# Last combine of a two-layer transformer kernel: the first expert's product moved to ScalarE, the first sum to GpSimd, for three of four tiles

## What is computed

```python
x = x + _L1_ffn_ref(_layernorm(x, axis=-1), L1_ffn_W1, ..., L1_ffn_br)
# in it:
h = jax.nn.gelu(jnp.einsum('td,edp->etp', xf, W1) + b1[:, None, :])
y = jnp.einsum('etp,epd->etd', h, W2) + b2[:, None, :]
out = jnp.einsum('te,etd->td', router_weights, y)
```

## Time and profile before

| What | Value |
|---|---|
| median of 3 runs | 548.41 us |
| the profiled execution, whole | 552.02 us |
| its span, first to last instruction | 550.3 us |
| PE / DVE / ACT / POOL busy | 87% / 70% / 39% / 54% |
| first last-combine instruction starts | 537.31 us |
| last last-combine instruction starts | 547.66 us, lasts 0.35 us |

### The profile page before, as it was taken

How to read it: one execution, slowest core, us unless ns; L and a number is a source line. 1 busy time by engine, 2 the same in 40 slices (tenths; PEclk the granted TensorE clock), 3 DMA queues, 4 the chain that set the end, 5 groups by cost and what they waited for, 6 DMA issues and landing times.

```text
span 550.3 us, 11816 instructions
## 1 busy us (share of the span) xinstructions
PE 478.7 (87%) x3625; PEld 429.6 (78%) x3625; DVE 387.1 (70%) x1304; ACT 215.9 (39%) x503; POOL 296.6 (54%) x310
## 2 busy tenths in 40 slices
PE   7658999999999697898777999999999789999950
PEld 6447998899987587788655988888888689989950
DVE  3655899888874435555358899999999546666637
ACT  3525666555652433333233343434434114333320
POOL 5346578888844224555523457676675623545440
PEclk9979999999999979999898999999999979999985
DMA  7999950000004622221020001010000012222117
GB/s 212 365 331 358 367 190 20 16 16 20 22 20 138 252 62 70 67 65 57 25 68 10 20 21 31 29 35 16 16 16 20 20 49 70 58 66 65 47 33 213
DMA packets 42931, 49.18 MB, mean 89 GB/s; under 512 B 7809, under 2 KB 28636, under 8 KB 42871
## 3 DMA queue, kind: packets, MB, share of 16 engines
q1 hardware_dynamic: 36991, 39.57, 22.8%
q0 software_dynamic: 4544, 8.44, 4.7%
q10 hardware_dynamic: 1336, 0.43, 0.4%
HBM read 20.97 MB, written 28.35 MB: 90 GB/s over the span
## 4 chain that ended last, share of the span: by engine, by line
PE 59%; POOL 12%; DVE 11%; issue 5%; DMA 3%; ACT 3%; SPq 2%; another core or an unknown queue 2%; POOLq 0%; DVEq 0%; ACTq 0%
PE ps L1581 12%; PE ps L1592 9%; POOL qr L498 5%; PE ps L1542 5%; PE ps L1519 5%; POOL rows L491 4%; PE ps L1496 3%; PE ps L1571 3%; PE ps L1447 3%; PE ps L1534 2%; PE ps L1544 2%; PE ps L1275 2%; PE ps L1360 1%; PE ps L1510 1%
## 5 line engine op out<-in xcount | busy, mean ns | idle before, releaser
L545 POOL DMA_INDIRECT ys<-ysbs,xs x78 | 77.8, 998 | 101.4 <-DVE ysbs L1233 43.0
L1581 PE MATMUL ps<-xsT,wups 128*128 128x128 f32 x624 | 87.1, 284 | 2.3 <-DVE big L1216 2.3
L1581 PEld LDWEIGHTS ps<-xsT,wups 128*128 128x128 f32 x624 | 78.8, 198 | 3.3 <-ACT xsT L717 2.4
L498 POOL TENSOR_TENSOR qr<-qsm,mhalf 128x16 f32<-128x16 f32 x16 | 47.5, 2966 | 3.0 <-DVE qsm L853 2.9
L491 POOL DMA_INDIRECT rows<-pays,slots x32 | 33.8, 1055 | 24.6 <-DVE slots L994 17.2
L519 POOL DMA_INDIRECT rows<-pays,slots x32 | 32.7, 1022 | 20.3 <-DVE slots L1059 14.5
L510 POOL TENSOR_TENSOR pp<-pp,rden 128x1232 f32<-128x1232 f32 x16 | 36.0, 2251 | 13.6 <-DVE x L1037 10.2
L730 ACT ACTIVATE big<-big 128x512 f32<-128x512 f32 x39 | 24.6, 630 | 46.8 <-PE ps L1592 23.8
L1592 PE MATMUL ps<-w2b,big 128*128 x312 | 41.1, 275 | 0.0
L1447 PE MATMUL ps<-region_a,pp 128*128 128x90 f32 (+1 forms) x320 | 39.6, 279 | 0.2
L1216 DVE TENSOR_TENSOR big<-big,ps 128x256 f32<-128x256 f32 x39 | 16.3, 417 | 33.1 <-PE ps L1592 18.9
(11 more groups left out here) (268 smaller groups left out, 1204.8 us busy)
## 6 DMA issues: line engine op xcount, KB each, us to landing
rows<-empty SPq DMA_DIRECT2D x68, 258.0 KB, 4.3
xs<-rows SPq DMA_DIRECT2D x78, 64.5 KB
region_b<-in_L_ffn_W_dram SPq DMA_DIRECT2D x2, 1024.0 KB, 9.8
region_a<-in_L_ffn_W_dram SPq DMA_DIRECT2D x1, 2048.0 KB
yb_all<-ys SPq DMA_DIRECT2D x16, 128.0 KB, 2.0
keys<-ys SPq DMA_DIRECT2D x8, 256.0 KB
ys<-ysbs,xs POOLq DMA_INDIRECT x78
rows<-pays,slots POOLq DMA_INDIRECT x64
```

What stands on the lines that cost most here:

```text
L498: pool.tensor_tensor(qr[s], qsm[s], mhalf[:, 0:H], ALU.pow).then_inc(a["qr"], 1)
L545: pool.indirect_dma_start(ys[l][:, :], bass.IndirectOffsetOnAxis(xs[j % XB][:, D:ROW].bitcast(I32), 0), ysb[j % YB], None, bounds_check=2 ...
L1581: ins = mm(S[s][:, k * P:(k + 1) * P], wup[t % WB][:, k * P:(k + 1) * P], xsT[s], start=True, stop=True)
```

## The change

For tiles t with t % 4 != 0 (12 of 16: 1, 2, 3, 5, ...), ScalarE multiplies y0 by g0 in place (an activation Copy with a per-partition scale), GpSimd adds the product to x in place, and VectorE does only the second of its two instructions, waiting for GpSimd. For tiles 0, 4, 8 and 12 VectorE does both, as before, except that the intermediate sum is put into x and not into y0.

```diff
@@ gpsimd, after the experts of both layers
+            m = M[1]
+            for t in range(NT):
+                if t % 4 != 0:
+                    pool.wait_ge(m["fscale"], m.count("fscale", t - t // 4))
+                    pool.tensor_tensor(x[:, t, :], x[:, t, :], ylast[t // 2][:, t % 2, 0, :], ALU.add).then_inc(m["fsum"], 1)
@@ scalar, after the experts of both layers
+            m = M[1]
+            act.wait_ge(m["gates"], m.count("gates", 3))
+            for t in range(NT):
+                if t % 4 != 0:
+                    act.wait_ge(xs_in[t // 2], 16 * (2 * ring_uses(t // 2) + 1))
+                    y0 = ylast[t // 2][:, t % 2, 0, :]
+                    act.activation(y0, y0, ACT.Copy, scale=gate[:, 0, t:t + 1]).then_inc(m["fscale"], 1)
@@ vector
-                dve.scalar_tensor_tensor(y0, y0, gate[:, 0, t:t + 1], x[:, t, :], ALU.mult, ALU.add).then_inc(m["fin0"], 1)
-                dve.wait_ge(m["fin0"], m.count("fin0", t + 1))
-                dve.scalar_tensor_tensor(x[:, t, :], y1, gate[:, 1, t:t + 1], y0, ALU.mult, ALU.add).then_inc(m["fin"], 1)
+                if t % 4 == 0:
+                    dve.scalar_tensor_tensor(x[:, t, :], y0, gate[:, 0, t:t + 1], x[:, t, :], ALU.mult, ALU.add).then_inc(m["fin0"], 1)
+                    dve.wait_ge(m["fin0"], m.count("fin0", t // 4 + 1))
+                else:
+                    dve.wait_ge(m["fsum"], m.count("fsum", t - t // 4))
+                dve.scalar_tensor_tensor(x[:, t, :], y1, gate[:, 1, t:t + 1], x[:, t, :], ALU.mult, ALU.add).then_inc(m["fin"], 1)
```

More of the change, by code:

```diff
@@ L288, in bass_xattn_moe_two_layers @@
         again.update({n: (moe0[n], c) for n, c in ONCE.items()})
-        M = [moe0, Stage("m", MOE + list(ONCE) + ["fin", "fin0"], again)]
+        M = [moe0, Stage("m", MOE + list(ONCE) + ["fin", "fin0", "fscale", "fsum"], again)]
         pro = Stage("p", PRO0)
```

## The result

| | before | changed |
|---|---|---|
| median, first measurement (4 runs each) | 548.98 us | 554.89 us |
| the profiled execution, its span | 550.3 us | 552.6 us |
| first last-combine instruction | 537.31 us | 538.08 us |
| end of VectorE's last instruction | 548.01 us | 547.75 us |
| so the combine takes | 10.70 us | 9.67 us |

The ratio is 1.0112, 95% interval [1.0068, 1.0156]: slower, where 2.1 us faster was forecast, and outside the range. Two later measurements of the same kernel gave 1.0039 [1.0003, 1.0074] and 1.0044 [1.0021, 1.0066], so its cost is rather 2 us than 6. The profiled execution takes 554.69 us, 2.09 more than its span; in the kernel before 1.72 us lay around the span.

A forecast was written before the change was run, and what follows sets the result against it. The end was taken as one serial chain, set by VectorE's 10.70 us last combine. Combine end 545.65, last landing 547.75 and 0.45 gave 548.2 against 550.3; 2.1 us off the median 548.41 gave 546.3 us, range 544.9 to 548.7.

The forecast's parts named there:

- the tail: After VectorE's last instruction: last output issue, 1.8 us to landing, about 0.45 us to span's end, 2.3 us together.
- the sums: GpSimd's additions of the products in the last combine: 12 at 0.454 us each, 5.45 us in a row.
- the hops: Handovers between engines in the combine: 0.15 us from ScalarE to GpSimd, 0.04 us from GpSimd back to VectorE.
- the hold-ups: GpSimd and VectorE hindering each other in the combine: 0.05 to 0.06 us a sum, 0.5 us in all.
- GpSimd's chain: GpSimd's queue from the third pair at 540.0, nine sums left: combine ends at 545.15, with hold-ups 545.65.
- The second rival: Hold-ups in the combine eat most of the gain, 0.17 us per sum and VectorE instruction: 547.6 us, chance 0.15.
- The third: GpSimd and VectorE take turns in the combine, 0.80 us a tile in place of 0.65: 550.0 us, chance 0.08.
- The 0.17 us: Delay of a VectorE instruction begun inside a GpSimd sum of the same shape: 0.58 us instead of 0.415.
- The arrival of the input: Transfers into the combine: input as good as arrived at 543.0 to 543.2, last pair of tiles about 543.1.
- The product: ScalarE's 128x128 multiplication by a per-partition column in the combine: 0.39 us each, 12 needing 4.7 us.
- The first output: Sign in the profile after: SP issues it within 0.1 us of the same place as before.
- The outputs' backlog: Outputs queued behind inputs at the end empty at 0.7 us each or quicker; last landing taken as 547.75.

The follow-up runs named there:

- e1: The changed kernel, its block closed without GpSimd's final drain; ratio to the kernel before 0.9983 [0.9953, 1.0013].
- e2: The kernel before plus a one-column GpSimd memset that waits for VectorE's last instruction; ratio to the kernel before 1.0087 [1.0055, 1.0118].
- e5: The kernel before, closed without GpSimd's final drain; ratio to the kernel before 0.9993 [0.9972, 1.0014].
- e7: The changed kernel plus a GpSimd drain between its last indirect DMA and first sum; ratio to the kernel before 0.9995 [0.9970, 1.0020].
- e4: The changed kernel with no edit, measured again; ratio to the kernel before 1.0039 [1.0003, 1.0074].
- e10: The changed kernel with no edit, measured a third time; ratio to the kernel before 1.0044 [1.0021, 1.0066].
- e8: The changed kernel with only the odd tiles offloaded and no final GpSimd drain; ratio to the kernel before 0.9975 [0.9957, 0.9994].

## Why the prediction was wrong

**The step that failed is the tail.** The prediction put behind VectorE's last instruction "the last issue, its 1.8 us to landing, and about 0.45 us to the span's end", and for GpSimd it counted the sums, the hops and the hold-ups. It costed what stands behind the new wait on VectorE and SP, and not what stands behind the new last instruction on GpSimd. That is the drain, 6.24 us, and it was free as long as GpSimd ended at 533.3. From the rows on record the sum would have been: last sum's end 545.3 + 6.24 + about 0.2 = 551.7 against 550.3, so +1.4 us; the stretches measured are 0.8 to 1.5 us longer, and 0.3 us lie outside the span. e1, e2, e5 and e7 show this step: the tail, 4.85 us in place of the 2.3 in the sum.

**VectorE's hold-ups were mis-sized.** The term was 0.5 us on GpSimd's chain, 0.05 to 0.06 a sum, and none on VectorE behind it. GpSimd does pay 0.05 us a sum, but from 0.41, so that a sum costs 0.46 where 0.454 + 0.055 was forecast. VectorE gets one instruction into each sum's time, 1.80 us for four in place of 1.14. So it ends 547.75 - 546.16 = 1.59 us behind the last sum, where 0.39 was in the sum, and the combine takes 9.67 us and not 8.34. The last sum ended 8.08 us behind the combine's start, 7.95 by the forecast; that is luck in part, since GpSimd had to wait 0.77 us for the fourth pair's product, which is not in the chain of the forecast, and the sums behind it were cheaper than forecast. The second rival had VectorE's price nearly right (0.17 us an instruction, measured 0.19) and charged the same to each sum, which was too much. The third did not come: the engines overlap, and a tile cost 0.46 us and not 0.80. The 0.17 us was not as good a source as it looked: the instruction of rows 11 has one input of tile size and not two, and rows 12, which have the two-input form, show 0.35 beside a larger sum.

**The arrival of the input sets much of the combine.** ScalarE starts on the last pair 6.67 us behind the combine's start in the first trace, 6.51 in e1, 6.39 in e4 and 5.88 in e10, and the combine takes 9.67, 9.55, 9.11 and 8.64 us. The forecast had 5.8. So without the tail the gain in the combine would have been 1.0 us in the first trace and up to 2.1 in the best, near the 2.4 of the forecast (10.70 - 8.34) but not by its working: in e10 the last sum ended 7.3 us in, 0.6 before the forecast, and VectorE 1.3 us behind it and not 0.39.

The Trainium skill (SBUF — State Buffer, section Who interferes with whom) says that a VectorE instruction with two SBUF inputs contends with a GpSimd instruction that reads SBUF, and not with one that only writes it. Both halves agree with the runs: 1.80 us for four beside sums, 1.14 beside memsets. The Trainium skill also calls this, in the same section, an exclusive lock, and lets the order of issue decide who blocks. The runs don't show such a lock: GpSimd's sums leave hardly a gap, and VectorE's instructions run inside them all the same, at 0.46 us each. Nor does one engine alone pay, though most of it falls on VectorE.

**What held.** The product took 0.401 us (0.39 forecast). ScalarE's first product ended at 538.46 and GpSimd started at 538.54, 0.08 us (0.15 forecast). The first output was issued at 539.54 against 538.08, 1.46 us into the combine, 1.42 before (538.73 - 537.31). The outputs' backlog did not bind: the last one took 1.8 us.

**What stays open.** The first ratio, 1.0112, is 6 us; the stretch accounts for 1.5 and the time outside the span for 0.4, and the two repeats gave 2.1 and 2.3. The pair of traces can't settle the rest, since the profiled execution of the kernel before took 552.02 us and not 549, and no trace of its quicker executions there was taken. In eleven traces of the experiments the combine starts anywhere from 514.8 to 518.2 us, in whatever kernel. This scatter goes with TensorE's granted clock: over the 34 executions of the kernel before beside e5 to e8, 0.01 less of it goes with 2.8 us more (correlation -0.88). The changed kernel was granted 0.935 to 0.947 in the four executions of the first measurement, 0.947 to 0.956 in e4 and 0.943 to 0.957 in e10. In the profiled one the mean was 0.92 up to 200 us and 0.95 from there to 450, in the kernel before 0.97 and 0.97 (the lower of its two levels, 1.2 GHz, held for 58 us ahead of the combine against 35); yet its combine starts only 0.77 us later. The clocks of the kernel before's quicker executions are not on record. So a lower clock in the first measurement is the likely reason, argued and not shown, and nothing here tells whether the change had a part in it.

## What to carry to other kernels

Work that is moved to the end of an engine's queue drags behind it what closes that queue: read the rows of the closing barrier before moving anything there, and keep GpSimd's last instruction, if it has issued indirect DMAs, 6.2 us ahead of the end, or drain it in an earlier idle time. Before work is given to GpSimd to relieve VectorE, ask what VectorE's own instructions cost beside it. And try first the order of VectorE's instructions: two that need each other cost 0.65 us back to back and 0.53 with another between them (1.05 us for two such pairs).

## What the runs showed of the hardware

- GpSimd's drain, in kernels where it has issued indirect DMAs, ended 6.21 to 6.23 us behind its last instruction in nine traces (6.18 to 6.28 as the rows show it), whether that was an indirect DMA, a sum or a memset of one column, and also where, as in e2, GpSimd had done nothing for 14 us after its last indirect DMA. A second drain, with twelve sums and no DMA behind the first, ended 0.07 us behind.
- A VectorE instruction with two SBUF inputs of 128x128 has a pace of 0.27 us alone, 0.38 when it waits for the one before it, and 0.46 beside GpSimd sums that read SBUF; beside memsets it keeps 0.27. GpSimd's sums start 0.41 us apart alone and 0.46 beside it.
- A product of 128x128 by a per-partition column on ScalarE, SBUF to SBUF, took 0.401 us, and two in a row 0.69 us.
